# Four tiles of lead instead of three for the gathered sums of a graph layer, with five slots of means

## The chip, the cores and the metric

The kernel runs on one core of a Trainium2 chip. The metric is the device time of one execution in microseconds (us). Times of the kernel before are the median of three runs. The profile is of one further execution, and its times in the trace are counted from the first instruction (the span).

## The reference, cut to what matters

N = 6250 rows of 512 features, E = 100000 edges sorted by destination (about 16 edges a row). Rows are taken in T = 49 tiles of 128, the last one of 106 rows.

```
xn  = layernorm(x)
agg = segment_sum(xn[src], dst) / max(degree, 1)          # mean of the neighbours
x   = x + xn @ W1.T + b1 + agg @ W2.T + b2 + linear_attention(xn)
x   = x + two_of_eight_experts(layernorm(x))              # gates from one pooled row
```

The linear attention needs, for every head, a sum over all rows of relu(k) times the row, before any row can be queried. The experts are chosen by one softmax over all rows after every row has its x. So there are three passes over the rows: the k loop, the layers, the experts.

## The kernel before, in words

**The k loop** (TensorE from L702, iterations i = -1 to T + 1) normalizes tile i, turns it with a DMA transpose into `xT` (ScalarE, L970, issued two iterations ahead), computes k of tile i (12 matmuls, `three`, L549 to L554) and adds tile i - 2 into four PSUM banks (12 matmuls, L708 to L710). The normalized rows go in two fp16 halves, 2 KB a row, to `table` in HBM. The fp16 rows of the last four tiles lie in buffers of their own (`natural`, L305 to L309).

**The gather.** Edges are cut into 782 blocks of 128 in the order of their destinations. When the table is stored, POOL issues 784 indirect DMAs (`fetch`, L520 to L523, two of them without edges), one a block, each of 128 rows of 2 KB, into `ring`, which has 16 slots. Slots come in groups of U = 4. POOL waits for `released` before the first gather of a group; TensorE gives it when it has added the group that lay in these slots. SyncE tells TensorE of a group that has landed (`arrived`, L411 stands near it).

**The aggregate** of a tile multiplies each block by a one-hot matrix of its destinations (VectorE, L1238) and adds it to the bank `ps_agg`, two matmuls of 128x512 a block (L622, L623 in `group`), about 17 blocks a tile. Edges of a block can belong to two tiles, so neighbours share a block and a group. VectorE then takes the degree (L1268, L1271) and ScalarE stores the mean in a slot of `ah` (`keep_ah`, L957 to L961), where it stays until the layer that uses it.

**Order of the aggregates.** `EARLY` names iterations of the k loop in which TensorE aggregates a tile: tiles 0, 1, 2 in iterations 39, 42, 45, each spread over that iteration and the two behind it. Tile `SKEW` = 3 is aggregated between the k loop and the layers, in the stretch in which the attention's matrix is made. From then on layer i aggregates tile i + skew.

**The layers** (`layer` in each engine's block, called by `layers`, L119): layer i queries tile i (12 matmuls, L742 to L747), turns the mean and the attention rows of tile i - 1 (L793, L800), does its three products (36 matmuls, L549 to L554) and turns the normalized result of tile i - 2 (L838). The groups of the aggregate stand between these, at five places. `LAYERS` lists runs of layers with their skew. Layers 12, 24 and 36 have None: they aggregate nothing, and the skew falls by one there, 3, 2, 1 and at last 0. `layers` puts runs into loops with a body of SLOTS layers and writes the rest out.

**The experts** follow the last layer and do not touch the gather.

The steps that the prediction names: `SKEW`, `SLOTS`, `EARLY`, `LAYERS` (L43 to L86), `layers` (L119 to L132), `x_end` (L196), `natural` (L305), `keep_ah` and its call in the k loop (L1017), the wait for `turned_ah` before the load into `x_end` (L1075), and the wait before `ksb` is overwritten (L1361).

Of the kernel before, what the change touches and what calls it, by code (L numbers as in the profile page):

```python
# [15 lines left out]
F32, F16, I32, U32, I16 = mybir.dt.float32, mybir.dt.float16, mybir.dt.int32, mybir.dt.uint32, mybir.dt.int16  # L16
# [10 lines left out]
T = (N + P - 1) // P  # L27
# [12 lines left out]
FULL = BLOCKS // P  # L40
XI = 6
NS = 4
SKEW = 3  # L43
OFF = 4
LEAD = 4
G4 = 4
# [26 lines left out]
def after(eng, sem, count):  # L73

    if not isinstance(count, int) or count > 0:
# [4 lines left out]
WK, WV, PJ, WQ, G1, G2 = range(6)  # L80
EDGES = 37
KP = 26
SLOTS = 4
EARLY = {39: 0, 42: 1, 45: 2}
LAYERS = ((1, 4, 3), (4, 12, 3), (12, 13, None), (13, 24, 2), (24, 25, None), (25, 36, 1), (36, 37, None), (37, T, 0),
          (T, T + 3, None))  # L86


STEPS = {i: [(PJ, i + 1)] for i in range(-1, 3)}
# [29 lines left out]
def layers(eng, body):  # L119

    for lo, hi, skew in LAYERS:
        a, b = -(-lo // SLOTS), hi // SLOTS
        if lo < 4 or b <= a:
            a = b = hi // SLOTS + 1
        for i in range(lo, min(a * SLOTS, hi)):
            body(i, skew, i % SLOTS)
        if b > a:
            with eng.Fori(a, b) as g:
                for k in range(SLOTS):
                    body(g * SLOTS + k, skew, k)  # L130
            for i in range(b * SLOTS, hi):
                body(i, skew, i % SLOTS)  # L132


def program(nc, x, src, dst, gw1, gb1, gw2, gb2, qkv_w, proj_w, proj_b, attn_w, attn_b, gate_w, gate_b,
            w1, b1, w2, b2, out):
    ctx = ExitStack()
    with ctx:
# [49 lines left out]
        work = sb("work", [P, 13, D], F32)  # L188
# [4 lines left out]
        k32, khl = work[:, 4], [work[:, b].bitcast(F16) for b in (5, 6, 12)]  # L193
        x2, xn2, acc, pT_, x_in, w32, ahT_ = (work[:, k] for k in range(7))
        ah = work[:, 7:7 + SLOTS]
        x_end = ah[:, (T - SLOTS) % SLOTS]  # L196
        ahT, pT = (v.bitcast(F16).rearrange("p (a c n) -> p a c n", a=2, c=C) for v in (ahT_, pT_))
        pre = work[:, 0:4].rearrange("p (b e) f -> p b e f", b=2)
        act2 = work[:, 4:8].rearrange("p (b e) f -> p b e f", b=2)
# [6 lines left out]
        awb = sb("awb", [P, D], F32)  # L206
# [98 lines left out]
        def natural(t):  # L305

            if t < T - NS:
                return xT[:, t + OFF].rearrange("p a n -> p (a n)")
            return (ksb[:, :], work[:, 10], work[:, 11], awb[:, :])[t - (T - NS)].bitcast(F16)  # L309

        def stored(eng, t):

            if t >= 0:
                eng.wait_ge(row_stored[t % NS], 16 * (t // NS) + 16 * len(parts(P if t < T - 1 else TAIL)))
# [591 lines left out]
        def _(act):  # L906
# [50 lines left out]
            def keep_ah(t, k):  # L957

                act.wait_ge(s["rd_made"], t + 1)
                after(act, s["turned_ah"], t - SLOTS + 1)  # L960
                F(ah[:, k % SLOTS, :], ps_agg[:, :], ACT.Copy, scale=rd[:]).then_inc(s["ah_made"], 1)  # L961
# [43 lines left out]
            for i in range(-1, T):  # L1005
                for kind, c in STEPS.get(i, ()):
                    prepare(done, kind, c)
                    done += 1
                if i >= 0:
                    turn(i + 2)  # L1010
                    act.wait_ge(s["k_made"], i + 1)
                    after(act, s["klo_made"], i)
                    F(k32, k_bank(i)[:, :], ACT.Relu, scale=SK).then_inc(s["k32_made"], 1)  # L1013
                    after(act, s["g_made"], i - 2)
                    F(khl[i % 3][:, 0:D], k_bank(i)[:, :], ACT.Relu, scale=SK).then_inc(s["khi_made"], 1)  # L1015
                if i - 2 in EARLY:
                    keep_ah(EARLY[i - 2], EARLY[i - 2])  # L1017
                for n in norm_slots(i):
                    normalize(n)
                if i in (4, 6):  # L1020
                    k = {4: G1, 6: G2}[i]
                    less_last(raw_w[k], (w_loaded[k], 16), s["weights_ready"], bcol[:, 0, :, None] if k == G1 else None)
                if i in (11, 12):
                    act.wait_ge(s["edges_loaded"], 144)
                    to, from_ = ((f_dst, raw_dst), (f_src, raw_src))[i - 11]
                    F(to, from_, ACT.Copy).then_inc(s["floats_made"], 1)
# [16 lines left out]
            def layer(i, skew, k):  # L1043
                t = i - 3
                if real(t):
                    after(act, s["turned_x2"], t + 1)
                    F(tile(t)[:, 0:C, :], ps_tx[:, :].rearrange("p (c n) -> p c n", c=C), ACT.Copy).then_inc(s["x2T_hi"], 1)
                t = i - 2
                if real(t):
                    after(act, s["mv2_made"], t + 1)  # L1050
                    after(act, s["rs2_made"], t)
                    F(std, mv[:, 1:2], ACT.Sqrt, bias=epsc[:], scale=1.0 / (SX * SX)).then_inc(s["std2_made"], 1)  # L1052
                t = i - 1
                if real(t):
                    after(act, s["turned_ah"], t + 1)
                    F(ahT[:, 0], ps_ta[:, :].rearrange("p (c n) -> p c n", c=C), ACT.Copy).then_inc(s["ahT_hi"], 1)
                    after(act, s["turned_p"], t + 1)
                    F(pT[:, 0], ps_tp[:, :].rearrange("p (c n) -> p c n", c=C), ACT.Copy, scale=SP_).then_inc(s["pT_hi"], 1)
                t = i - 2
                if real(t):  # L1060
                    after(act, s["negm_made"], t + 1)
                    F(e2[:], sm[:], ACT.Exp, bias=negm[:]).then_inc(s["exp_made"], 1)
                    after(act, s["exp_made"], t + 1)
                    after(act, s["acc_made"], t)
                    F(acc, acc, ACT.Copy, scale=e2[:, 0:1]).then_inc(s["accs_made"], 1)
                    after(act, s["x2_stored"], 16 * t)
                    after(act, s["x2_made"], t + 1)
                    act.dma_start(x2_dram[bass.ds(t * P, P), :], x2).then_inc(s["x2_stored"], 16)
                    if isinstance(t, int) and t == T - 1:
                        act.wait_ge(s["best_made"], 1)  # L1070
                        F(wp[:], negm[:], ACT.Exp, bias=gst[:, 1:2], scale=-1.0).then_inc(s["wp_made"], 1)
                t = i - 1
                if real(t):
                    if isinstance(t, int) and t == T - 2:
                        act.wait_ge(s["turned_ah"], T - SLOTS + 1)  # L1075
                        for a, b in parts(TAIL):
                            act.dma_start(x_end[a:b, :], x[(T - 1) * P + a:(T - 1) * P + b, :]).then_inc(s["x_end_loaded"], 16)
                    if not (isinstance(t, int) and t == T - 1):
                        after(act, s["sraw_made"], t)
                        after(act, s["x_loaded2"], 16 * t)  # L1080
                        act.dma_start(x_in, x[bass.ds(t * P, P), :]).then_inc(s["x_loaded2"], 16)
                if skew is not None:
                    keep_ah(i + skew, k + skew)
# [50 lines left out]
        def _(dve):  # L1134
# [223 lines left out]
            V.tensor_tensor(vtm, bank[0][:, :].rearrange("p (a f) -> p a f", a=C),  # L1358
                            hmask[:, None, :].to_broadcast([P, C, P]), ALU.mult).then_inc(s["vtm_made"], 1)
            dve.wait_ge(s["ksum_made"], 1)  # L1360
            stored(dve, T - NS)  # L1361
            link(V.tensor_scalar(ksb[:], bank[4][:, :], mix[:, 0:1], None, ALU.mult))
            dve.sem_inc(s["ksb_made"], 1)
            link(V.tensor_scalar(kinv[:], bank[3][:, 0:C], SX * 1e-30, None, ALU.max))
# [303 lines left out]
```

## Time and profile before

| what | us |
|---|---|
| median of 3 runs | 1580.96 |
| lowest, highest | 1580.53, 1581.2 |
| the profiled execution | 1580.07 |
| its span in the trace | 1578.3 |
| mean granted TensorE clock | 0.989 |
| gathers issued by POOL, first to last | 209.14 to 1268.45 |
| busy: TensorE, VectorE, ScalarE, POOL | 1519.8, 1003.1, 604.5, 799.0 |

The k loop runs until about 327 us, the layers from there to about 1287 us, the experts from about 1310 us to the end. Lines of the trace give an engine, a line of the kernel, the operation, what it writes and reads, and in square brackets the engine's idle time before it with what ended that. Matmuls overlap, so that a matmul shown with 0.38 us is followed by the next after 0.22 us; distances between starts are the times to read.

### The profile page before, as it was taken

What the parts mean: (1) busy time and instruction counts of PE and PEld (TensorE: products, weight loads), DVE (VectorE), ACT (ScalarE), POOL (GpSimd) and SP (SyncE); (2) the same over time, 40 slices, a digit from 0 to 9 for tenths busy, and PEclk for the clock granted to TensorE, in tenths of its full rate; (3) what the DMA queues carried; (4) which work ended last, traced back from release to release, by engine and by line L of the source; (5) the groups of instructions that cost most, each with busy time, mean ns of one, the idle gap of its engine ahead of it and who ended that gap; (6) DMA issues with size and microseconds to landing.
All of it is one profiled execution on the core that took longest, in us unless ns stands there. A gap on an engine that the chain in (4) does not pass through costs nothing.

```text
span 1578.3 us, 29172 instructions
## 1 busy us (share of the span) xinstructions
PE 1519.8 (96%) x7597; PEld 733.7 (46%) x7598; DVE 1003.1 (64%) x2154; ACT 604.5 (38%) x997; POOL 799.0 (51%) x847
## 2 busy tenths in 40 slices
PE   5999999989999999999999999999999989999997
PEld 2444444444544444444444444444544444444443
DVE  7576522246666667666677666666666666666777
ACT  5777721111333333332333333333333335555554
POOL 4122143646777767777767777767777710000000
PEclk8999999999999999999999999999999989999998
DMA  9977776957777767777767777767777723322323
GB/s 237 262 170 190 189 179 132 217 151 208 234 235 234 234 209 231 234 234 237 233 206 239 239 240 233 234 209 236 236 233 233 233 80 120 107 90 96 106 87 112
DMA packets 166610, 308.64 MB, mean 196 GB/s; under 512 B 71986, under 2 KB 74572, under 8 KB 166260
## 3 DMA queue, kind: packets, MB, share of 16 engines
q0 software_dynamic: 62720, 205.57, 44.3%
q1 hardware_dynamic: 36112, 58.90, 11.7%
q10 hardware_dynamic: 67684, 42.96, 10.7%
q8 instruction: 53, 0.87, 0.2%
q14 instruction: 41, 0.34, 0.1%
HBM read 255.02 MB, written 39.49 MB: 187 GB/s over the span
## 4 chain that ended last, share of the span: by engine, by line
PE 70%; POOL 14%; issue 6%; DVE 3%; DMA 1%; ACT 0%; DVEq 0%; SPq 0%; ACTq 0%
POOL ring L522 14%; PE bank L549 13%; PE bank L554 13%; PE bank L550 12%; PE bank L622 8%; PE bank L623 8%; PE bank L708 2%; PE bank L709 2%; PE bank L710 2%; PE bank L742 2%; PE bank L747 2%; PE bank L743 2%; PE bank L793 1%; PE bank L838 1%; PE bank L800 1%
## 5 line engine op out<-in xcount | busy, mean ns | idle before, releaser
L522 POOL DMA_INDIRECT ring<-table,src_col x784 | 753.5, 961 | 328.9 <-issue 254.5
L622 PE MATMUL bank<-ring,onehot 128*128 x830 | 316.1, 381 | 14.8 <-issue 6.2
L623 PE MATMUL bank<-ring,onehot 128*128 x830 | 315.5, 380 | 0.0
L1238 DVE TENSOR_TENSOR onehot<-bank,dst_col 128x512 f32 x244 | 168.8, 692 | 96.5 <-issue 61.1
L961 ACT ACTIVATE work<-bank,rd 128x512 f32<-128x512 f32 x49 | 33.7, 687 | 336.4 <-DVE rd L1271 336.3
L549 PE MATMUL bank<-wts,xT 128*128 128x512 f16 x392 | 149.1, 380 | 4.1 <-DVE wts L1313 4.1
L550 PE MATMUL bank<-wts,xT 128*128 128x512 f16 x392 | 149.0, 380 | 0.0
L549 PE MATMUL bank<-wts,work 128*128 128x512 f16 x392 | 148.2, 378 | 0.2 <-DVE work L1441 0.2
L550 PE MATMUL bank<-wts,work 128*128 128x512 f16 x392 | 148.3, 378 | 0.0
L622 PEld LDWEIGHTS bank<-ring,onehot 128*128 x830 | 80.9, 97 | 126.5 <-issue 45.6
L623 PEld LDWEIGHTS bank<-ring,onehot 128*128 x830 | 81.1, 98 | 84.8 <-issue 0.9
L554 PE MATMUL bank<-wts,xT 128*128 128x512 f16 x392 | 101.5, 382 | 0.0
L554 PE MATMUL bank<-wts,work 128*128 128x512 f16 x392 | 100.6, 379 | 0.0
L1052 ACT ACTIVATE std<-mv,epsc 128x1 f32<-128x1 f32 x49 | 14.4, 295 | 222.6 <-DVE mv L1437 222.6
L1268 DVE TENSOR_SCALAR dg<-bank 128x1 f32<-128x1 f32 x49 | 7.7, 158 | 137.2 <-PE bank L610 137.2
L1118 ACT ACTIVATE work<-work 128x512 f32<-128x512 f32 x98 | 61.8, 630 | 79.9 <-DVE work L1622 78.8
L509 POOL TENSOR_TENSOR work<-work 128x512 f16<-128x512 f32 x27 | 31.7, 1176 | 119.8 <-ACT work L1015 119.8
L1013 ACT ACTIVATE work<-bank 128x512 f32<-128x512 f32 x49 | 29.2, 596 | 136.0 <-PE bank L554 131.6
L1622 DVE SCALAR_TENSOR_TENSOR work<-bank,mix,work 128x512 f32<-128x512 f32 x98 | 69.9, 747 | 15.1 <-PE bank L554 9.8
L1612 DVE SCALAR_TENSOR_TENSOR ring<-work,gexp,ring 128x512 f32 (+1 forms) x98 | 73.3, 748 | 8.9 <-DVE ring L1612 3.8
L549 PE MATMUL bank<-xT,wts 128*128 (+2 forms) x208 | 75.0, 367 | 3.1 <-ACT wts L1096 3.1
L708 PE MATMUL bank<-work,xT 128*128 128x512 f16 x180 | 69.6, 386 | 6.0 <-POOL work L509 6.0
(284 smaller groups left out, 2732.5 us busy)
## 6 DMA issues: line engine op xcount, KB each, us to landing
ring<-table,src_col POOLq DMA_INDIRECT x784, 3.7
x_rows<-work ACTq DMA_DIRECT2D x49, 256.0 KB, 3.7
work<-in_x ACTq DMA_DIRECT2D x48, 256.0 KB, 4.3
ring<-x_rows SPq DMA_DIRECT2D x12, 1024.0 KB, 5.3
out_x<-ring SPq DMA_DIRECT2D x12, 1024.0 KB
table<-xT SPq DMA_DIRECT2D x45, 256.0 KB, 3.5
ring<-in_x SPq DMA_DIRECT2D x42, 256.0 KB, 3.7
xT<-in_L_mix_qkv_weight SPq DMA_DIRECT2D x2, 1024.0 KB, 10.1
```

What stands on the lines that cost most here:

```text
L522: pool.indirect_dma_start(ring[:, n, :], None, table[:, :], bass.IndirectOffsetOnAxis(ap=ap, axis=0)).then_inc(slot_loaded[n], 16)
L549: mm(out_, wh(c), mh(c), start=first and c == 0, stop=False)
L550: mm(out_, wh(c), ml(c), start=False, stop=False)
L554: r = mm(out_, wl(c), mh(c), start=False, stop=last and c == n - 1)
L622: mm(ps_agg[:, :], w[:, k, :], rows[:, k, 0:D], start=start, stop=False, skip_group_check=True)
L623: r = mm(ps_agg[:, :], w[:, k, :], rows[:, k, D:2 * D], start=False, stop=stop, skip_group_check=True)
L708: mm(bank[c][:, :], xs[:, c * P:(c + 1) * P], kh, start=(t == 0), stop=False)
L961: F(ah[:, k % SLOTS, :], ps_agg[:, :], ACT.Copy, scale=rd[:]).then_inc(s["ah_made"], 1)
L1118: F(act2[:, j % 2, e], pre[:, j % 2, e], ACT.Gelu).then_inc(s["act_made"], 1)
L1238: V.tensor_tensor(onehot[:, bass.ds((q + t) % OG * U, U), :], ps_iota[:, None, :].to_broadcast([P, U, P]), dst_col[:, bass.ds(q % GROUPS * ...
L1612: r = V.scalar_tensor_tensor(out=y, in0=act2[:, j % 2, e], scalar=gexp[:, e:e + 1], in1=y, op0=ALU.mult, op1=ALU.add)
L1622: V.scalar_tensor_tensor(out=pre[:, j % 2, e], in0=bank[4 + 2 * (j % 2) + e][:, :], scalar=mix[:, 4:5], in1=b2b[:, e], op0=ALU.mult, op1=A ...
```

## The change

The lead of the aggregates over the layers becomes four tiles. `SLOTS` is 5. The k loop aggregates four tiles, 0 to 3, in iterations 36, 39, 42 and 45; tile 4 takes the place of tile 3 behind the k loop. Layers 14, 25, 36 and 47 have no aggregate. `layers` now begins a loop at the first layer of a run, not at a multiple of SLOTS, and makes one of any run with at least two whole bodies. The fourth early mean lies in `work[:, 10]`, where the row buffer of tile T - 4 = 45 was and is: tiles 45 and 46 change buffers, so ScalarE waits for the store of tile 45 before that mean, and VectorE for that of tile 46 before it overwrites `ksb`. `x_end` stays the slot of tile 45.

```diff
-SKEW = 3
+SKEW = 4
...
-SLOTS = 4
-EARLY = {39: 0, 42: 1, 45: 2}
-LAYERS = ((1, 4, 3), (4, 12, 3), (12, 13, None), (13, 24, 2), (24, 25, None), (25, 36, 1), (36, 37, None), (37, T, 0),
-          (T, T + 3, None))
+SLOTS = 5
+EARLY = {36: 0, 39: 1, 42: 2, 45: 3}
+LAYERS = ((1, 4, 4), (4, 14, 4), (14, 15, None), (15, 25, 3), (25, 26, None), (26, 36, 2), (36, 37, None), (37, 47, 1),
+          (47, 48, None), (48, T, 0), (T, T + 3, None))
...
     for lo, hi, skew in LAYERS:
-        a, b = -(-lo // SLOTS), hi // SLOTS
-        if lo < 4 or b <= a:
-            a = b = hi // SLOTS + 1
-        for i in range(lo, min(a * SLOTS, hi)):
+        n = (hi - lo) // SLOTS
+        if n > 1:
+            with eng.Fori(0, n) as g:
+                for k in range(SLOTS):
+                    body(g * SLOTS + lo + k, skew, (lo + k) % SLOTS)
+            lo += n * SLOTS
+        for i in range(lo, hi):
             body(i, skew, i % SLOTS)
-        if b > a:
-            with eng.Fori(a, b) as g:
-                for k in range(SLOTS):
-                    body(g * SLOTS + k, skew, k)
-            for i in range(b * SLOTS, hi):
-                body(i, skew, i % SLOTS)
...
-        x_end = ah[:, (T - SLOTS) % SLOTS]
+        x_end = ah[:, (T - 4) % SLOTS]
...
-            return (ksb[:, :], work[:, 10], work[:, 11], awb[:, :])[t - (T - NS)].bitcast(F16)
+            return (work[:, 10], ksb[:, :], work[:, 11], awb[:, :])[t - (T - NS)].bitcast(F16)
...
                 if i - 2 in EARLY:
+                    if EARLY[i - 2] == SKEW - 1:
+                        stored(act, T - NS)
                     keep_ah(EARLY[i - 2], EARLY[i - 2])
...
-                        act.wait_ge(s["turned_ah"], T - SLOTS + 1)
+                        act.wait_ge(s["turned_ah"], T - 3)
...
-            stored(dve, T - NS)
+            stored(dve, T - NS + 1)
             link(V.tensor_scalar(ksb[:], bank[4][:, :], mix[:, 0:1], None, ALU.mult))
```

## Rows read from the trace of the kernel before

**Rows 1.** The page: busy us (share) and instructions; L522's group: busy, mean ns.

```profile
PE 1519.8 (96%) x7597; PEld 733.7 (46%) x7598; DVE 1003.1 (64%) x2154; ACT 604.5 (38%) x997; POOL 799.0 (51%) x847
...
L522 POOL DMA_INDIRECT ring<-table,src_col x784 | 753.5, 961 | 328.9 <-issue 254.5
```

**Rows 2.** Windows: busy PE, PEld, DVE, ACT, POOL (instructions), clock, DMA share, GB/s.

```profile
209.00:230.00 21.00, 21.00 (x99) 9.51 (x97) 2.77 (x4) 4.34 (x8) 16.28 (x16) 1.00 0.93 229
...
520.00:560.00 40.00, 38.66 (x200) 18.74 (x199) 26.52 (x59) 12.04 (x18) 30.25 (x33) 1.00 0.77 233
560.00:600.00 40.00, 39.98 (x205) 19.64 (x204) 27.77 (x63) 15.01 (x23) 26.21 (x28) 1.00 0.68 206
...
574.50:586.20 11.70, 11.70 (x63) 6.11 (x61) 9.14 (x22) 6.02 (x9) 8.11 (x9) 1.00 0.74 231
```

**Rows 3.** Timeline of POOL: start us, duration us, instruction, idle time before it.

```profile
229.12 0.94 POOL L522 DMA_INDIRECT ring<-table,src_col  x1 [0.30 <-issue]
253.12 0.94 POOL L522 DMA_INDIRECT ring<-table,src_col  x1 [23.06 <-PE bank L610]
...
277.07 0.94 POOL L522 DMA_INDIRECT ring<-table,src_col  x1 [4.26 <-PE bank L610]
...
338.45 0.94 POOL L522 DMA_INDIRECT ring<-table,src_col  x1 [17.94 <-PE bank L610]
...
362.13 0.94 POOL L522 DMA_INDIRECT ring<-table,src_col  x1 [3.90 <-PE bank L610]
...
590.92 0.94 POOL L522 DMA_INDIRECT ring<-table,src_col  x1 [5.87 <-PE bank L610]
...
819.34 0.94 POOL L522 DMA_INDIRECT ring<-table,src_col  x1 [5.86 <-PE bank L610]
...
1046.69 0.94 POOL L522 DMA_INDIRECT ring<-table,src_col  x1 [6.64 <-PE bank L610]
...
1268.45 0.94 POOL L522 DMA_INDIRECT ring<-table,src_col  x1 [0.30 <-issue]
```

**Rows 4.** Timeline of TensorE: first query matmuls of layers 12 to 15, 23, 24, 48.

```profile
574.49 0.38 PE L742 MATMUL bank<-wts,xT 128*128 128x512 f16 x1
...
586.16 0.38 PE L742 MATMUL bank<-wts,xT 128*128 128x512 f16 x1
...
605.55 0.38 PE L742 MATMUL bank<-wts,xT 128*128 128x512 f16 x1
...
624.82 0.38 PE L742 MATMUL bank<-wts,xT 128*128 128x512 f16 x1
...
782.81 0.38 PE L742 MATMUL bank<-wts,xT 128*128 128x512 f16 x1
...
802.91 0.38 PE L742 MATMUL bank<-wts,xT 128*128 128x512 f16 x1
...
1259.86 0.38 PE L742 MATMUL bank<-wts,xT 128*128 128x512 f16 x1
```

**Rows 5.** Waits of TensorE's weight loads, 362 to 1270 us: total, times, longest.

```profile
PEld bank L622 <- issue: 34.6, 77, 1.5
```

**Rows 6.** Timeline of TensorE in the k loop: iterations, first blocks of two tiles.

```profile
231.09 0.38 PE L708 MATMUL bank<-work,xT 128*128 128x512 f16 x1
...
236.27 0.38 PE L708 MATMUL bank<-work,xT 128*128 128x512 f16 x1
...
275.34 0.38 PE L622 MATMUL bank<-ring,onehot 128*128 x1
...
298.60 0.38 PE L622 MATMUL bank<-ring,onehot 128*128 x1
```

**Rows 7.** The DMA transposes of L970: one issue, who waited for them, their landing.

```profile
239.19 1.25 ACTq L970 DMA_TRANSPOSE xT<-xT  x1
...
PEld bank L549: 4.3, 1
...
DMA to landing us min/median/max: 3.1/4.8/10.5
```

## The prediction

> **What bounds the kernel now.** I read the page first [rows 1]: TensorE is busy for 1519.8 of 1578.3 us, POOL for 799, nearly all of it in 784 gathers. Such a TensorE share does not say which of the two sets the pace, so I went on to the windows [rows 2]. Between 520 and 560 us TensorE shows a little idle time and POOL issues 33 gathers; between 560 and 600 us TensorE is full and POOL issues 28. The two take turns.
>
> The starts of the layers settle it [rows 4]. A layer is the stretch between two first query matmuls (L742). The layer from 605.55 to 624.82 took 19.27 us with an aggregate of 17 blocks, with no idle time in it. The layer without an aggregate, 574.49 to 586.16, took 11.67 us. The layer of 17 blocks from 782.81 to 802.91, the last before a gap, took 20.10 us: there TensorE waits in small pieces [rows 5].
>
> The gathers [rows 3] explain the 20.1. Read the start and the idle time before it (0.30 us is normal). The 81st gather starts at 362.13, the 257th at 590.92 and the 784th at 1268.45. The waits at 590.92, 819.34 (5.86, the same pattern) and 1046.69 exceed that by 5.57, 5.56 and 6.34 us. So 176 gathers took 228.8 - 5.6 = 223.2 us, 1.268 each, and the next 527 took 677.5 - 11.9 = 665.6 us, 1.263 each; 1.2645 over all. A tile needs 16 new gathers: 20.2 us, against 19.3 us of TensorE. In the layers **the gather is the slower by 1.0 us a tile**. The ring holds 16 blocks, so POOL cannot bank more than one tile. A gap layer gives it 11.7 us, of which it idles 5.6 with the ring full: 6.1 us banked, enough for about six layers. After that TensorE runs at 20.2 us until the next gap. Each of the present runs has 11 or 12 layers, so each ends bound by the gather.
>
> **The change part by part.**
>
> *One more tile in the k loop.* An iteration of the k loop takes 236.27 - 231.09 = 5.18 us, three take 15.54. Three with a tile in them take 298.60 - 275.34 = 23.26 [rows 6], so a tile costs 7.7 us of TensorE there. Tile 0 now starts at iteration 36, at 236.27, instead of 39. The first 16 gathers were issued by 229.12 + 0.94 [rows 3], so its rows have landed, and POOL's wait of 23.06 us before the 17th gather falls to about 7.5. The end of the k loop comes 7.7 us later, and so does the point of [rows 3] where POOL starts to run without waits (362.13 before, 369.8 now). The waits between (4.26, a like one, 17.94 and 3.90) stay, with one more small one, because each is tied to a step of TensorE, and there are now 96 gathers behind that point and not 80. On the gather's account that is 16 x 1.2645 - 7.7 = **12.5 us ahead** of before.
>
> *The layers.* Aggregates in layers go from 45 to 44, gap layers from three to four; the number of layers stays. TensorE's own work changes by +7.7 in the k loop and 11.7 - 19.3 = -7.6 in the layers: nothing. The runs between gaps are now 13, 10, 10, 10 and 1 layers. The first four are all longer than the six which the bank covers, so each still ends on the gather, and its three gaps (14, 25, 36) still idle POOL 5.6 to 6.3 us each: no change against the three before. So tile 47 is summed 12.5 us earlier than now. Today that is the start of layer 48, at 1259.86 [rows 4]. Then comes the new part: that sum now ends layer 46, and layer 47 is the fourth gap, **11.67 us** in which the last eight or so gathers come in and nobody waits. Layer 48 starts at 1259.9 - 12.5 + 11.7 = 1259.1, 0.8 us earlier than before. From there on everything is what it was: one aggregate with skew 0, the tail, the experts.
>
> *A fuller ring at an awkward tile.* Tiles do not start on a group of four blocks. By the destinations that the reference draws, tile 30 starts on the last block of its group, so that group's slots are freed one query later than usual. It now comes in the third full layer after a gap and not in the fifth, when the ring is fuller. The trace has no such wait (the waits of [rows 3], with the one like 277.07, are all that POOL shows): from below 0, from above 2 us, what is left of the 6.1 us bank's first two layers. I take 1.0, the middle, since both ends are equally near.
>
> *Five slots and the loops.* The means get a fifth tile of SBUF; x_end and the row buffers of tiles 45 and 46 change places. The slot is waited for at the same layer as before (turned_ah >= i). Loop bodies are of five layers and not four, with four back edges as before. Their control work sits behind eight matmuls of a group, as now (layers in loops and outside both take 19.27); bounds 0 and 0.5 us, taken 0. The wait for the store of tile 45 before the fourth mean is on ACT, in front of the normalizing queue of the k loop, but the store went out long before: 0. Vector and ScalarE in the gap: 9.14 and 6.02 us of 11.7 [rows 2], so TensorE still closes that layer: 0. If that cover went, the p transposes of the next layer would be late.
>
> *Pitch.* In the k loop 16 gathers went from 253.12 to 277.07 with 3.96 us of waiting, 1.249 each, against 1.2645 in the layers. I leave the moved 16 at the layers' pitch. The Trainium skill, "SBUF — State Buffer", section "SBUF: two separate sides", says that POOL cannot write a DMA's descriptors while VectorE holds the shared port pair, so a gather beside less VectorE work is quicker. By that rule the sum would be 0.2 us less; the trace agrees in the sign.
>
> **Sum:** -0.8 + 1.0 = +0.2 us on the profiled execution's 1580.07 us (its span of 1578.3 and 1.8 around it). The median of the runs, 1580.96, is 0.9 above that one, so I forecast 1581.1 us. That is no change: about 0.2% (3.2 us) is what a measurement of this kernel can tell from none.
>
> **The rivals.**
>
> *Late transposes, slower.* The gathers of tile 1 now run from 237 us, beside the DMA transposes of xT that the k loop needs two iterations later. A transpose landed after 4.8 us in the median and 10.5 at most, and one held TensorE for 4.3 us [rows 7]; the one issued at 239.19 us is used by the k matmuls of iteration 39, at 236.27 + 2.5 x 5.18 = 249.2 us, so 10 us are there [rows 6, 7]. For it: the DMA engines are 93% busy where both run, between 209 and 230 us. Against it: TensorE was busy for all of these 21 us, with the same 16 gathers and the same transposes [rows 2]. It decides from a landing of 10 us on. The price is one such wait, 4.3 us, which goes onto the end in full: 1585.4 us. The Trainium skill, "Trainium Kernel Development and Optimization", section "Key Constraints", says that DMAs of all queues run on the same 16 DMA engines and interleave, which speaks for this rival; the trace shows both sides of it. Chance 0.10.
>
> *The waits go, faster.* If the extra lead carried on as a lead, TensorE would never wait in the layers. From gap to gap, 574.49 to 802.91, are 228.4 us, of which 11.67 + 11 x 19.3 = 224 are work: 4.4 us of waits a run, 18 in four runs, so 1563 us. Against it: the bank is the ring, and the skew does not enlarge it; the waits return after six layers whatever the skew. Chance 0.03.
>
> *Another pitch.* Of the 688 gathers behind the restart each follows the pitch one to one. The two stretches above differ by 0.005 us, which is 3.4 us on the sum. At the low end the time is 1577.7, at the high end 1584.5. Chance beyond either end 0.06 each.
>
> *The fourth gap is wasted in full.* If the three other gaps left more in the bank than they do (runs of 10 layers that end before the gather binds), POOL idles more in each. It would take a bank of ten layers: three times up to 4 us. The eleven-layer runs show waits in their last five or six layers, so at most 0.05, ending near 1585.
>
> **How the numbers follow.** The forecast's case (the gather's account with its 12.5 against 11.7) has 0.70, the rivals 0.10, 0.03, 0.12 and 0.05. Faster by over 0.2% (under 1577.8): 0.03, the low end of the pitch 0.06 and 0.04 of the forecast's case, 0.13. Slower by over 0.2% (over 1584.1): 0.06 of the 0.10, 0.06 and 0.03, and 0.02 of the forecast, 0.17. Same: 0.70. The range takes in the pitch, the bounds of 0 to 2 and the 4.3 us: 1577.0 to 1585.4.
>
> **What would show it.** The 17th gather starts near 237.5 us; the run without waits starts near 369.8 with the 97th gather. Layer starts L742: 7.7 us later than now in layers 1 to 6, gap 14 near 622, the last gap near 1247, layer 48 within 2 us of 1259.9. POOL idles 5 to 7 us in three gaps and not in the fourth; its last gather starts 10 to 12 us earlier, near 1257. Layers late in each run still take 20.1 us. It would be wrong if layers of 17 blocks took 19.3 us throughout, if POOL showed new waits outside these places, or if L549 waited for a transpose in the k loop.

## The result and the profile after

The changed kernel takes 1589.71 us in the median of five runs (1588.79 to 1593.67), the kernel before 1581.2 us beside it: a ratio of 1.0056, with an interval from 1.0042 to 1.007. It is slower by 8.5 us, and the forecast of 1581.1 us (1577.0 to 1585.4) does not hold it. The profiled execution took 1589.14 us with a span of 1586.5 us, 9.07 us more than the one of before.

The first lines of its page answer to [rows 1]:

```profile
PE 1518.3 (96%) x7597; PEld 734.3 (46%) x7598; DVE 1003.9 (63%) x2154; ACT 604.7 (38%) x997; POOL 796.5 (50%) x847
...
L519 POOL DMA_INDIRECT ring<-table,src_col x784 | 751.1, 958 | 326.3 <-issue 253.0
```

The work is the same on every engine: TensorE is busy for 1.5 us less in a span that is 8.2 us longer. So the time is in waits. (Up to L1016 the lines of the kernel are numbered three lower than before, and behind it one lower: L742 is L739 now, VectorE's L1271 is L1270.)

The timeline of TensorE answers to [rows 4]: the first query matmuls of layers 9, 10, 14, 15, 20, 47 and 48.

```profile
520.81 0.38 PE L739 MATMUL bank<-wts,xT 128*128 128x512 f16 x1
...
548.08 0.38 PE L739 MATMUL bank<-wts,xT 128*128 128x512 f16 x1
...
625.70 0.38 PE L739 MATMUL bank<-wts,xT 128*128 128x512 f16 x1
...
637.37 0.38 PE L739 MATMUL bank<-wts,xT 128*128 128x512 f16 x1
...
733.82 0.38 PE L739 MATMUL bank<-wts,xT 128*128 128x512 f16 x1
...
1255.63 0.38 PE L739 MATMUL bank<-wts,xT 128*128 128x512 f16 x1
...
1267.30 0.38 PE L739 MATMUL bank<-wts,xT 128*128 128x512 f16 x1
```

Layer 48 starts at 1267.30, 7.4 us later than before and 8.2 later than forecast. The gap layers are as expected (14 and 47 take 11.67 us). Layer 9 is not: it takes 27.27 us, where an 18-block layer without waits takes 19.7. Layer 20, from 733.82, takes 25.13 us in the same way. Only layers 0 and 1 take as long (23.6 and 26.0 us, in the kernel before 23.5 and 26.1); from layer 2 on no layer of before takes over 21.1 us.

The waits in the layers, 362 to 1270 us, answer to [rows 5]. Columns: total us, times, longest.

```profile
PEld bank L619 <- issue: 42.2, 67, 6.2
...
PE bank L619 <- DVE onehot L1237: 11.7, 5, 6.0
```

The first row was 34.6 us before; 5.5 of the 7.6 us more are a wait of layer 1 that falls into this window now and stood ahead of it then. The second row is new: in the kernel before, no row of TensorE's matmuls ends on VectorE's one-hots; now 11.7 us do. So I read VectorE's timeline at the head of layer 9 and at that of layer 20:

```profile
520.52 0.16 DVE L1267 TENSOR_SCALAR dg<-bank 128x1 f32<-128x1 f32 x1 [2.73 <-PE bank L607]
520.72 0.16 DVE L1270 RECIPROCAL rd<-dg 128x1 f32<-128x1 f32 x1
526.91 0.75 DVE L1418 SCALAR_TENSOR_TENSOR work<-bank,mix,work 128x512 f32<-128x512 f32 x1 [6.03 <-issue]
...
733.73 0.16 DVE L1270 RECIPROCAL rd<-dg 128x1 f32<-128x1 f32 x1
737.55 0.75 DVE L1418 SCALAR_TENSOR_TENSOR work<-bank,mix,work 128x512 f32<-128x512 f32 x1 [3.66 <-issue]
...
944.86 0.17 DVE L1270 RECIPROCAL rd<-dg 128x1 f32<-128x1 f32 x1
945.61 0.75 DVE L1418 SCALAR_TENSOR_TENSOR work<-bank,mix,work 128x512 f32<-128x512 f32 x1 [0.59 <-issue]
```

Between the reciprocal that ends one layer and the first operation of the next, VectorE stands for 6.03 us, then 3.66 us, then (the third such place) 0.59 us. "issue" says that no semaphore was awaited. What lies there is the backward branch of VectorE's loop (branches and register work are in the trace, but not in this view): the trace has it at 520.80 and at 733.82, and the next instruction starts 3.14 and 3.35 us after it ended. At 520.80 there are two stops: three short instructions follow the first, and then nothing for another 2.64 us. The kernel before shows 0.62 us at the same place:

```profile
493.39 0.16 DVE L1271 RECIPROCAL rd<-dg 128x1 f32<-128x1 f32 x1
494.17 0.75 DVE L1419 SCALAR_TENSOR_TENSOR work<-bank,mix,work 128x512 f32<-128x512 f32 x1 [0.62 <-issue]
```

The DMA view of after, for 518 to 530 us, names what moved meanwhile (packets, MB, share of 16 engines); the same view of 936 to 948 us, around the branch that doesn't stall, has no such queue:

```profile
q0 software_dynamic: 813, 2.65, 76.0%
q14 instruction: 3, 0.02, 0.5%
```

These are three transfers of 8192 bytes of instructions, at 522.19, 525.15 and 528.46 us; at the other branch there are two, at 735.44 and 738.82. The first starts 1.3 us after the branch, and VectorE goes on 1.5 us after it has landed; the second answers to the second stop in the same way. The view names a queue and not an engine, so this is a reading so far: VectorE jumped back to instructions that it no longer held and had to have them fetched again. Experiments 7, 10 and 11 test it. TensorE's aggregate of layer 9 then waits for its one-hot. The same place on TensorE's timeline, and the windows (busy PE, PEld, DVE, ACT, POOL, granted clock, DMA share, GB/s):

```profile
530.90 0.60 PE L619 MATMUL bank<-ring,onehot 128*128 x1 [5.95 <-DVE onehot L1237]
```

```profile
528.00:538.00 10.00, 7.09 (x28) 3.00 (x29) 7.40 (x14) 2.55 (x4) 5.61 (x6) 0.71 0.52 149
538.00:548.10 10.10, 10.10 (x55) 4.89 (x54) 5.44 (x16) 1.02 (x2) 7.71 (x8) 1.00 0.84 258
```

There is a second price. After those 6 us of rest the granted clock is 0.71 over 528 to 538 us, a mix of the 2.4 and the 1.2 GHz level, where the kernel before has 1.00, and the first aggregate matmul takes 0.60 us instead of 0.38. A wait of 5.95 us goes with a layer that is 7.55 us longer, and in layer 20 a wait of 3.57 us with one that is 5.4 us longer (granted clock 0.83 over 738 to 748 us).

POOL's timeline answers to [rows 3]: the 17th gather, the restart at the 97th, a new wait in layer 9, gap 14, a new wait in layer 20, gap 25, the wait of tile 30, gap 36, and the last gather.

```profile
238.04 0.94 POOL L519 DMA_INDIRECT ring<-table,src_col  x1 [7.52 <-PE bank L607]
...
370.24 0.94 POOL L519 DMA_INDIRECT ring<-table,src_col  x1 [3.89 <-PE bank L607]
...
534.51 0.94 POOL L519 DMA_INDIRECT ring<-table,src_col  x1 [3.13 <-PE bank L620]
...
642.13 0.94 POOL L519 DMA_INDIRECT ring<-table,src_col  x1 [6.91 <-PE bank L607]
...
744.93 0.94 POOL L519 DMA_INDIRECT ring<-table,src_col  x1 [2.13 <-PE bank L620]
...
853.18 0.94 POOL L519 DMA_INDIRECT ring<-table,src_col  x1 [7.07 <-PE bank L607]
...
889.95 0.94 POOL L519 DMA_INDIRECT ring<-table,src_col  x1 [1.66 <-PE bank L607]
...
1062.78 0.94 POOL L519 DMA_INDIRECT ring<-table,src_col  x1 [6.51 <-PE bank L607]
...
1264.04 0.95 POOL L519 DMA_INDIRECT ring<-table,src_col  x1 [0.30 <-issue]
```

Up to the restart everything is where the forecast had it (238.04 against "near 237.5", 370.24 against 369.8). After that the gathers themselves lose time, because a TensorE that stands frees no ring slots: 2.8 us beyond the usual 0.30 at 534.51 and 1.8 us at 744.93. New waits of POOL outside the places it named were one of the prediction's own signs of being wrong.

### The profile page after: what moved, and what is told of

It reads as the page before. It is cut to its first block, busy times and chain, and to the rows that moved or that the text cites. A ratio compares the mean times of both kernels' runs of the same rounds, so it can differ in the third digit from the quotient of the medians.

```text
span 1586.5 us, 29392 instructions
## 1 busy us (share of the span) xinstructions
PE 1518.3 (96%) x7597; PEld 734.3 (46%) x7598; DVE 1003.9 (63%) x2154; ACT 604.7 (38%) x997; POOL 796.5 (50%) x847
## 4 chain that ended last, share of the span: by engine, by line
PE 87%; DVE 3%; issue 2%; DVEq 1%; DMA 1%; ACT 0%; SPq 0%; ACTq 0%
PE bank L546 15%; PE bank L551 15%; PE bank L547 15%; PE bank L619 12%; PE bank L620 11%; PE bank L739 2%; PE bank L744 2%; PE bank L740 2%; PE bank L705 2%; PE bank L706 2%; PE bank L707 2%; PE bank L835 1%; PE bank L790 1%; PE bank L797 1%; DVE ring L1611 1%
## 5 line engine op out<-in xcount | busy, mean ns | idle before, releaser
L619 PE MATMUL bank<-ring,onehot 128*128 x830 | 317.5, 383 | 23.0 <-DVE onehot L1237 11.7
```

Source lines behind the costliest of these rows:

```text
L619: mm(ps_agg[:, :], w[:, k, :], rows[:, k, 0:D], start=start, stop=False, skip_group_check=True)
```

## The experiments

**What the theories are.** Theory A (F in the recorded expectations): the slowdown is VectorE's backward branch. Rival B (G there): the schedule itself (four tiles ahead, the fourth gap) costs more than I had counted. Rival C (H there): the loop bodies of TensorE or ScalarE, which also grew from four to five layers. The experiments are told by what they are about; there is no number 5. A ratio is always to the kernel before as it was measured beside that experiment (1581.2 to 1582.4 us), and times of layers are from one profiled execution each.

*Experiment 1. VectorE's layers written out, TensorE and ScalarE looped.*

```
-def layers(eng, body):
+def layers(eng, body, loops=True):
-        if n > 1:
+        if loops and n > 1:
...
-            layers(dve, layer)
+            layers(dve, layer, loops=False)
```

> The changed kernel, with VectorE's layers written out instead of looped; TensorE and ScalarE keep their loops. Theory F (VectorE stands 6.0 and 3.7 us at two branches back to the first layer of a five-layer body, while its instructions are fetched anew, and TensorE waits 7.6 and 5.4 us for one-hots in layers 9 and 20): both waits go, layer 9 takes about 19.7 us and not 27.3, layer 20 about 19.8 and not 25.1, the gather binds again late in each run, and the time is 1581 +-1.5 us, the 1581.1 of the prediction's own account. Rival G (the lead itself costs: fourth gap and fuller ring): the time stays at 1588 or more.

Measured: 1583.57 us, 1.001 of the kernel before (0.9999 to 1.002). The same work without a backward branch on VectorE is 6.1 us faster than the kernel after. That is 1 us above the range I gave: layers 9 and 20 take 20.87 and 20.47 us and not 19.7 and 19.8, because short waits for the gathers stand there now. Layer 48 begins at 1261.99:

```profile
1261.99 0.38 PE L739 MATMUL bank<-wts,xT 128*128 128x512 f16 x1
```

*Experiment 2. The opposite edit: TensorE and ScalarE written out, VectorE looped.*

```
-            layers(pe, layer)
+            layers(pe, layer, loops=False)
...
-            layers(act, layer)
+            layers(act, layer, loops=False)
```

> The changed kernel, with TensorE's and ScalarE's layers written out and VectorE's still looped over five. Theory F: the two VectorE stalls stay (6 and 4 us behind its backward branch), time 1588 to 1591 us. Rival H (it is the loops of TensorE or ScalarE that cost, VectorE only shows it): the time falls to about 1581.

Measured: 1590.35 us, 1.006 (1.0038 to 1.0082), like the kernel after. The six executions lie between 1586.3 and 1598.5, and the profiled one is the longest of them. VectorE's stops are still there, 3.53 us at 524.7 (with a second one behind it) and 3.42 us at 738.3. Rival C falls.

*Experiment 3. The kernel before with five slots of means and with the new loops, but still three tiles ahead.*

```
-SLOTS = 4
+SLOTS = 5
...
-        a, b = -(-lo // SLOTS), hi // SLOTS
+        n = (hi - lo) // SLOTS
...
```

> The kernel before (lead of three, three gaps, three tiles in the k loop) with five slots and the changed kernel's way of making loops: VectorE loops over five layers in the runs from 13, 25 and 37. Theory F: one or two of three backward branches stall VectorE 3 to 6 us with no change of the lead at all. How much reaches the end depends on the gather, which binds late in each run and hides a stall in part: 1582 to 1588 us. Rival G: 1581.2, as the kernel before.

Measured: 1583.05 us, 1.0012 (1.0002 to 1.0021). No branch of VectorE stalls, although its bodies have five layers and 316, 315 and 314 instructions. So "five layers to a body" is not yet the cause, and the expectation of one or two stalls failed; that the time lies in its range is luck. The layers lose 1.3 us (layer 48 begins at 1261.16 against 1259.86).

*Experiment 6, the control: the kernel before with VectorE written out.* The edit is that of experiment 1, on the kernel before.

> The kernel before with VectorE's layers written out and nothing else changed; TensorE's and ScalarE's loops stay. It is the control for the first experiment, where the same edit gave back 6.1 us to the kernel after. The four backward branches of VectorE cost 0.30 to 0.38 us each in the kernel before and nothing refetched there. Theory 'a loop body that VectorE must fetch again': nothing to win here, 1580 to 1583 us (a straight stream has to be fetched whole, so a small loss of 0 to 2 us is possible), and layer 48 begins at 1259 to 1262. Rival 'writing VectorE out is worth about 6 us in any kernel of this kind, whatever its branches do': 1575 us and layer 48 at about 1254.

Measured: 1581.17 us, 0.9996 (0.9987 to 1.0005); layer 48 begins at 1259.48. Writing VectorE out is worth nothing by itself, so the 6.1 us of experiment 1 are the stalls and not something that the edit brings along.

*Experiment 7. Why two branches of four?* The compiled program of VectorE settled the form of the question. An instruction has 64 bytes in it, so a transfer of 8192 bytes holds 128. The bodies that stalled are the first two, of 318 and 317 instructions; 316 and 315 did not. Either length decides (317 is too much), or the place in the stream does. To part them, 48 semaphore increments that nobody waits for move all four bodies and change none:

```
+        for _ in range(pads.get(lo, 0)):
+            eng.sem_inc(pad, 1)
...
-            layers(dve, layer)
+            layers(dve, layer, pad, {4: 48})
```

> The kernel after with 48 semaphore increments that nobody waits for, on VectorE, between layer 3 and the loop of layers 4 to 13. No loop body changes its length (318, 317, 316 and 315 instructions); each begins 48 instructions later in the stream: at 877, 1223, 1568 and 1912, that is at 109, 71, 32 and 120 in blocks of 128 instructions, which is what one of VectorE's instruction transfers of 8192 bytes holds. Theory 'place': the bodies seen so far that did not stall began at 72 to 116 of such a block and those that did at 23 and 61, which fits a store of three blocks of 128 whose edges lie some 62 to 72 instructions behind the start of the count, and a body that reaches into four of them is fetched again. Then the first two back edges (layers 8 to 9 and 19 to 20) cost 0.3 to 0.5 us as in the loops that do not stall, the third (layer 30 to 31) stalls for 3 to 6 us, the fourth does not; the time is 1585 to 1588 us. Theory 'length': 317 instructions and more do not fit and 316 do. Then the first two stall as in the kernel after (6.0 and 3.7 us in front of the first operation of the next layer), the third and fourth do not, and the time is 1589 to 1591 us.

The time was 1588.77 us, 1.0043 (1.0028 to 1.0058). VectorE's timeline at the three places:

```profile
530.11 0.75 DVE L1421 SCALAR_TENSOR_TENSOR work<-bank,mix,work 128x512 f32<-128x512 f32 x1 [0.56 <-issue]
...
738.23 0.75 DVE L1421 SCALAR_TENSOR_TENSOR work<-bank,mix,work 128x512 f32<-128x512 f32 x1 [0.59 <-issue]
...
952.31 0.75 DVE L1421 SCALAR_TENSOR_TENSOR work<-bank,mix,work 128x512 f32<-128x512 f32 x1 [4.36 <-issue]
```

The first two stalls are gone with bodies of unchanged length, and the third body, of 316 instructions, stalls now. Place decides. The time is a little over the range that I gave (1585 to 1588): the increments stand in front of layer 4, and that layer takes 27.27 us. The next run shows the same.

*Experiment 8. All four bodies placed well.* The edit of experiment 7 with 43, 20, 44 and 40 increments.

> The kernel after with 43, 20, 44 and 40 such increments on VectorE in front of its four loops, so that the bodies begin at 104, 86, 91 and 91 of their block of 128 and by the theory 'place' reach into three blocks each. Theory 'place': no back edge of VectorE takes over 0.5 us, layer 48 begins at 1260 to 1263 and the time is that of the kernel after with VectorE written out, 1582 to 1585 us (the increments themselves cost VectorE some 50 ns each, 2 us in front of a loop, where it has slack). Theory 'length': the back edges of layers 8 to 9 and 19 to 20 stall for 6 and 3.7 us and the time is 1589 to 1591 us.

No branch stalls (none takes over 0.4 us), and yet the time was 1590.19 us, 1.006 (1.0046 to 1.0074). The forecast of the time failed, and the trace says on what: the padding.

```profile
422.41 0.16 DVE L1273 RECIPROCAL rd<-dg 128x1 f32<-128x1 f32 x1
427.24 0.75 DVE L1421 SCALAR_TENSOR_TENSOR work<-bank,mix,work 128x512 f32<-128x512 f32 x1 [4.67 <-issue]
```

An increment takes VectorE 93 ns, not my 50, and at the head of layer 4 there is no slack: the layer takes 25.63 us, 6.4 more than one of 17 blocks without waits. The 20 to 44 increments behind the gap layers cost nothing of the kind: layer 15 takes 19.26 us, and layers 26 and 37 take 20.38 and 20.44, where experiment 7 has 20.42 and 19.83 without increments there. This is in fact a stall of VectorE made by hand, with the same effect as those of the branch.

*Experiment 10. The same places, with the first 43 increments where VectorE idles,* waiting for TensorE's matrix at 346 to 354 us.

```
+            for _ in range(43):
+                dve.sem_inc(pad, 1)
             for j in range(C):
                 dve.wait_ge(s["m_made"], j + 1)
...
-            layers(dve, layer)
+            layers(dve, layer, pad, {15: 20, 26: 44, 37: 40})
```

> The kernel after with its four loops on VectorE placed as in the eighth experiment (bodies from 103, 85, 90 and 90 of a block of 128 instructions), but the 43 increments that move the first loop stand where VectorE waits for TensorE's kernel matrix (it idled 7.6 us at 346 to 354 us in the kernel after) and not in front of layer 4, where 43 increments took 4.4 us at 93 ns each and TensorE lost 6.4 us in layer 4. Theory 'place of the loop body in VectorE's store of instructions': no stall at any back edge, layer 4 loses under 0.5 us, TensorE's waits in layers 2 to 47 sum to 20 to 21 us as with VectorE written out (20.5), layer 48 begins at 1261 to 1263, and the time is 1582 to 1585 us. Rival 'writing VectorE out took away something besides the stalls': layer 48 begins at 1264 or later and the time is 1586 us or more with no stall in the trace.

Measured: 1584.87 us, 1.0017 (1.0003 to 1.0031), all loops kept. TensorE and VectorE:

```profile
1261.51 0.38 PE L742 MATMUL bank<-wts,xT 128*128 128x512 f16 x1
```

```profile
522.25 0.75 DVE L1423 SCALAR_TENSOR_TENSOR work<-bank,mix,work 128x512 f32<-128x512 f32 x1 [0.58 <-issue]
...
730.57 0.75 DVE L1423 SCALAR_TENSOR_TENSOR work<-bank,mix,work 128x512 f32<-128x512 f32 x1 [0.60 <-issue]
```

Layer 48 begins at 1261.51, 5.8 us before that of the kernel after and within 0.5 us of the written-out one. Instructions that do nothing make the kernel faster, by moving a loop. What is left against the kernel before, 0.17% (0.03 to 0.31), is rival B's share: small, but not nothing.

*Experiment 11. Twice as many stalls: all four bodies placed badly.* 39 and 40 increments in front of the third and fourth loop only.

> The kernel after with 39 and 40 increments on VectorE in front of its third and fourth loop, which follow the layers without an aggregate, where VectorE has slack. The first two loops stand as in the kernel after (from 61 and 23 of their block of 128 instructions); the third and fourth, of 316 and 315 instructions, now begin at 23 too. Theory 'place': all four back edges stall, the third and fourth (layers 30 to 31 and 41 to 42) by 3 to 6 us on VectorE, of which TensorE loses 2 to 5 us each; the time is 1592 to 1597 us. Theory 'length' (316 instructions fit wherever they stand): the third and fourth do not stall, and the time is 1589 to 1591 us.

Measured: 1591.87 us, 1.0057 (1.0038 to 1.0076), just under the 1592 that I expected at least. Against experiment 10, measured beside it, that is 7.0 us more for four stalls. But the ratio is that of the kernel after (1.0056), so in the time the two further stalls don't show beyond the noise; they show in the trace. The third and fourth place, and the instruction transfers in 1156 to 1166 us:

```profile
952.50 0.75 DVE L1421 SCALAR_TENSOR_TENSOR work<-bank,mix,work 128x512 f32<-128x512 f32 x1 [4.25 <-issue]
...
1160.95 0.75 DVE L1421 SCALAR_TENSOR_TENSOR work<-bank,mix,work 128x512 f32<-128x512 f32 x1 [3.48 <-issue]
```

```profile
q14 instruction: 2, 0.02, 0.8%
```

All four stall. The two new ones make their layers 2.8 and 4.4 us longer than such layers are without waits; yet layer 48 begins only 2.9 us later than in the kernel after (1270.2). The layers behind a stall take 19.26 us again: the gathers have caught up, TensorE has no small waits there, and that gives back more than half.

All looped versions together, VectorE's bodies by start (counted from the stream's first instruction, modulo 128) and length, with a star where the branch stalled:

```
kernel                  first     second    third     fourth
before                  35/254    89/253    14/252    66/252
after (and 2)           61/318*   23/317*   112/316   72/315
experiment 3            93/316    105/315   116/314
experiment 7            109/318   71/317    32/316*   120/315
experiment 8            104/318   86/317    91/316    91/315
experiment 10           103/318   85/317    90/316    90/315
experiment 11           61/318*   23/317*   23/316*   23/315*
```

The increments do two things at once, they move the loop and they take time, but experiments 7 and 11 use them to bring a stall about and experiment 10 to take two away, and each came out by place. One rule fits all bodies of the table: VectorE still has the head of the body if the body touches at most three blocks of 128 instructions, and has to fetch it if the body touches four. The edges of the blocks must then lie 57 to 66 instructions ahead of multiples of 128 in this count. The double stop at 520.80 gives the edge independently: the body starts at 61, the three instructions at 61, 62 and 63 run, and the one at 64 has to wait, so an edge lies in front of 64. By this rule a body of 254, which touches three blocks at most wherever it stands, could not stall in the kernel before, and for 318 instructions only about half of the places (67 of 128) are good.

The Trainium skill has a rule for this, on the page "Runtime: NRT & Kernel Launch", section "Instruction fetch mechanics": an engine other than TensorE holds 512 instructions, refilled in blocks of 256 ahead of the sequencer, and a taken branch to a target outside that window has to wait for a DMA. The trace agrees with the mechanism. The size would fit too, if besides the three blocks a fourth is always arriving, which no run shows by itself. The block does not agree: the transfers behind VectorE's branches have 8192 bytes here, 128 instructions. With blocks of 256 the first two bodies, which start at 61 and 151 modulo 256, could not both have reached into a third.

*Experiment 4. The gaps spread evenly.* With VectorE written out, gap layers at 10, 20, 30 and 40 instead of 14, 25, 36 and 47. The runs between are now too short for two bodies of five, so `layers` makes no loop on TensorE and ScalarE either, here and in experiment 9 (experiment 2 gained nothing by that).

```
-LAYERS = ((1, 4, 4), (4, 14, 4), (14, 15, None), (15, 25, 3), (25, 26, None), (26, 36, 2), (36, 37, None), (37, 47, 1),
-          (47, 48, None), (48, T, 0), (T, T + 3, None))
+LAYERS = ((1, 4, 4), (4, 10, 4), (10, 11, None), (11, 20, 3), (20, 21, None), (21, 30, 2), (30, 31, None), (31, 40, 1),
+          (40, 41, None), (41, T, 0), (T, T + 3, None))
```

> The changed kernel with VectorE written out and the four layers without an aggregate at 10, 20, 30, 40 instead of 14, 25, 36, 47. By the gather's account a gap at 47 costs TensorE 11.7 us when there is hardly anything left to gather; at 40 it costs the gather only its 5.8 us of full ring, as the others do. Layer 48 would start 12.5 - 5.8 = 6.7 us before that of the kernel before: near 1253, time about 1574.5 us (+-1.5). If the account is wrong and TensorE's own work already binds, the time is as that of the variant with gaps at 14 to 47.

Measured: 1578.77 us, 0.9978 (0.9964 to 0.9993), and layer 48 at 1257.35, 4.6 us before that of experiment 1. It is faster than both kernels, but by less than forecast (1574.5 us, layer 48 near 1253). POOL's waits at the gaps of layers 20 and 40 are longer than the 5.8 us that I had counted:

```profile
743.42 0.95 POOL L519 DMA_INDIRECT ring<-table,src_col  x1 [9.01 <-PE bank L607]
...
1125.36 0.94 POOL L519 DMA_INDIRECT ring<-table,src_col  x1 [8.15 <-PE bank L607]
```

*Experiment 9. The gaps at 12, 22, 32 and 42,* the rest as in experiment 4.

> The kernel after with VectorE written out and the four layers without an aggregate at 12, 22, 32 and 42, where the fourth experiment had them at 10, 20, 30 and 40 (1578.8 us). There GpSimd idled 8.7 us at the gap of layer 20 and 8.0 us at that of layer 40, against 5.7 and 6.3 at the others: the gathers had not yet fallen far enough behind to use the 11.67 us. Theory 'a gap pays what the gathers are behind': with the gaps later by two layers GpSimd idles 5.5 to 7 us at each, layer 48 begins 1 to 3 us earlier than 1257.4, and the time is 1576 to 1578 us. Rival 'what counts is the length of the stretch after which the gathers hold TensorE up': the two extra layers ahead of the first gap bring 1 to 2 us of short waits (layers 10 and 11), the stretches between gaps are of nine layers in both, and the time stays within 1578 to 1580 us.

Measured: 1577.05 us, 0.9968 (0.9958 to 0.9978), the fastest of all. POOL at the four gaps:

```profile
598.72 0.94 POOL L519 DMA_INDIRECT ring<-table,src_col  x1 [6.04 <-PE bank L607]
...
786.71 0.95 POOL L519 DMA_INDIRECT ring<-table,src_col  x1 [6.57 <-PE bank L607]
...
975.61 0.94 POOL L519 DMA_INDIRECT ring<-table,src_col  x1 [6.73 <-PE bank L607]
...
1164.73 0.94 POOL L519 DMA_INDIRECT ring<-table,src_col  x1 [8.02 <-PE bank L607]
```

Only the second idle came down (from 9.01 us); the first and the third were low before, and the fourth is still 8.02. Layer 48 begins at 1257.22, only 0.13 us before that of experiment 4, not the 1 to 3 us that I expected, so that the time fell into its range is luck: the 0.1% between the ratios of experiments 4 and 9 lies inside their intervals. The rival's waits are there: layers 10 and 11 take 20.30 and 20.15 us, layers 20 and 21 21.40 and 20.55. So it seems that idle time which POOL is spared at a gap comes back to TensorE as short waits ahead of it, and POOL's long idles were not what experiment 4 lost. What both show against experiment 1 is that gaps placed earlier, the last with layers behind it, are worth 4.6 to 4.8 us at layer 48. All four gaps moved, so the share of the last alone is not shown.

## Why the prediction was wrong

**The step that failed** is "Five slots and the loops". It counted the back edges (four, as before) and what control work sits beside a group of matmuls, and took 0 with bounds of 0 and 0.5 us. It did not ask how long a body is in instructions, and whose. Its reason for 0, the matmuls that cover the control work, is one for TensorE's loop; for VectorE's it had none. VectorE's body grew from 254 to 318, which put the question of place where there had been none, and two of four bodies lay badly: two stops of 6.0 and 3.7 us, layers 9 and 20 longer by 7.55 and 5.4 us. With the small waits which those layers have anyway, and with what the gathers catch up meanwhile, that is 5.3 us at layer 48 by experiment 1 and 5.8 us by experiment 10. Without the stalls the time (1583.57 and 1584.87 us) lies inside the range, in its upper half.

**The rest by its steps.**

- *One more tile in the k loop:* layer 0 begins 7.7 us later in experiment 10 and 8.0 us later in the kernel after (334.8 and 335.0 against 327.1 us), the restart is at 370.24 where 369.8 was forecast. Right.
- *The layers:* in experiment 10, the change without its stalls, the last gather is at 1258.27, 10.2 us earlier than before, as "10 to 12" said. The fourth gap takes its 11.67 us, 1249.84 to 1261.51. Right.
- *Waits of POOL at three gaps and not at the fourth:* right; in experiment 10 they are 6.1, 6.1 and 6.0 us beyond 0.30, 18.2 in all where the three of before have 17.5. The kernel after has 6.6, 6.8 and 6.2.
- *A fuller ring at an awkward tile:* the wait exists at the tile named. In the kernel after it is 1.36 us beyond 0.30 (the row at 889.95), in experiment 10 2.1 (2.39 at 884.35), against 1.0 taken and 2 as the upper bound. Undersized.
- *The sum:* layer 48 without stalls is at 1261.5, against 1260.1 (1259.1 and that 1.0). By the gathers' account, the undersized wait is 1.1 of the difference, new small waits of POOL in layers 4, 27 and 38 are 0.6, 0.2 and 0.6, and the gaps are 0.7; the pitch of 1.2616 us against the 1.2645 used gives 1.9 back over 687 gathers. That leaves 1.3 us, which is what the last gather is late against the forecast (1258.27 against 1256.95), of the 1.4 us. (The rows of before give 888.8 us for 703 gathers, 1.2643 and not the 1.2645 of the prediction; on the 16 moved gathers that is nothing.)

So the profiled 9.07 us are: 5.3 to 5.8 of stalls, 1.6 to 2.1 of the schedule, 0.8 in the stretch from layer 48 to the end, and 0.87 outside the span (2.64 us against 1.77). The last two, from one execution each, are within what executions of one kernel differ by.

**The rivals.** Late transposes did not occur: no wait of the k matmuls stands in the k loop, and TensorE begins layer 0 one tile of work later. The waits in the layers did not go. The pitch stayed between the two ends. "The fourth gap is wasted in full" did not occur as it was told: it wanted POOL to idle up to 4 us more in each of the other three gaps, and there it idles as forecast. Experiments 4 and 9 show something else, that the schedule has better places for its gaps. The failed step was none of the rivals: no chance had been given to it.

## What to carry to other kernels

Before lengthening a loop body, count its instructions on each engine, not its time: a body is free at its back edge only while the engine still holds its head; here that held for VectorE's bodies that touch at most three blocks of 128 instructions. Where it is near that, the place of the loop in the stream decides, so an edit elsewhere can switch a stall on or off; read the first instruction after each backward branch, and look for an instruction transfer beside it. And look where a pause given to the slower engine stands: here the version with work behind its last pause was the faster one, though which of the four moved pauses did it was not parted.

## What the runs showed of the hardware

- A backward branch of VectorE to instructions that it holds costs 0.30 to 0.39 us until the next instruction; to instructions that it doesn't hold, 3.2 to 4.1 us (nine stalls), and 2.3 to 2.6 us more in the three cases in which the body starts three instructions ahead of a block's edge. The transfer of 8192 bytes in each stop takes 0.3 to 0.65 us itself, so most of the cost is the time before and behind it. The gathers keep the DMA engines 76% busy meanwhile (518 to 530 us); whether a stall is shorter without them was not tried.
- VectorE's straight stream of layers, which is fetched whole, costs nothing measurable: 0.9996 (0.9987 to 1.0005).
- TensorE's body has some 1560 instructions in the compiled program, and its back edges show no stall in any run that has them, nor do ScalarE's (0.24 us at most).
- A semaphore increment took VectorE 93 ns.
- The stretch from layer 48 to the end takes 317.7 to 321.8 us in the profiled executions, though the code there is the same. In experiment 3 it took 320.8 us (1582.0 - 1261.2) against 318.4 in the kernel before, with a granted clock of 0.64 in 8 us at the start of the experts' matmuls, where the kernel before had 1.00 (windows of experiment 3, then of before):

```profile
1313.00:1321.00 8.00, 7.77 (x24) 3.41 (x25) 3.85 (x12) 0.79 (x2) 0.00 (x0) 0.64 0.67 241
```

```profile
1312.00:1320.00 8.00, 7.53 (x34) 3.31 (x34) 6.13 (x21) 3.40 (x5) 0.00 (x0) 1.00 0.76 254
```

Each kernel has one profiled execution, so whether the clock's level there goes with the kernel or with the execution stays open. So does what sets the position of the block edges in the count.
